# Sums of squares of k and q as products with two constant columns

## What is computed

```
q = _short_conv(x @ Wq, qc_w).reshape(b, l, NH, DK)      # NH, DK = 4, 64; ends in silu
k = _short_conv(x @ Wk, kc_w).reshape(b, l, NH, DK)
beta = jax.nn.sigmoid(x @ Wb)

def _l2norm(x):
    return x * jax.lax.rsqrt(jnp.sum(x * x, -1, keepdims=True) + 1e-06)

def _delta_rule(q, k, v, beta, chunk=CHUNK):             # chunks of 32 tokens
    q = _l2norm(q)
    k = _l2norm(k)
    v = v * beta[..., None]
    kb = k * beta[..., None]
    A = -jnp.tril(jnp.einsum('bhncd,bhned->bhnce', kb, k), -1)
    T = solve_triangular(eye - A, ...)
    ...                                                  # scan over the chunks with the state S
```

## Time and profile before

| | us |
|---|---|
| median of 3 runs | 1182.75 (1180.84 to 1190.8) |
| the profiled execution, its device time | 1176.66 |
| its span in the trace | 1174.9 |
| PE busy | 1051.7 (90%) |
| DVE busy | 827.4 (70%) |
| ACT busy | 551.9 (47%) |

### The profile page before, as it was taken

The page is one execution under the profiler, slowest core; times in us unless marked ns, Lnnn a source line. Parts: engine busy times, 40 slices in busy tenths (PEclk is TensorE's granted clock), DMA queues, the critical chain, the costliest instruction groups (busy, mean ns, idle before and its releaser), DMA issues.

```text
span 1174.9 us, 25682 instructions
## 1 busy us (share of the span) xinstructions
PE 1051.7 (90%) x10348; PEld 785.6 (67%) x10348; DVE 827.4 (70%) x1620; ACT 551.9 (47%) x989; POOL 410.6 (35%) x648
## 2 busy tenths in 40 slices
PE   5858899899999999899998998899998999897738
PEld 4734785588637885488747885488747885486427
DVE  6584478875887668875887668875887668863373
ACT  2254348443564337533575337533574337542431
POOL 7228200951058200961048300771038300770000
PEclk9779799999998999999999999999998999995779
DMA  5140104020130203110140202110040202210000
GB/s 159 20 108 1 37 19 106 4 54 2 51 77 11 45 19 86 24 36 20 33 95 1 55 19 67 42 36 20 28 99 1 54 1 64 46 36 19 1 0 19
DMA packets 82933, 47.45 MB, mean 40 GB/s; under 512 B 58496, under 2 KB 76416, under 8 KB 82816
## 3 DMA queue, kind: packets, MB, share of 16 engines
q1 hardware_dynamic: 82816, 45.82, 16.8%
HBM read 31.12 MB, written 14.68 MB: 39 GB/s over the span
## 4 chain that ended last, share of the span: by engine, by line
PE 69%; DVE 16%; ACT 8%; POOL 3%; issue 3%; DMA 1%; SPq 0%; DVEq 0%; ACTq 0%; POOLq 0%
PE psum L814 14%; PE psum L815 13%; PE psum L816 13%; PE psum L845 6%; DVE arena L1695 4%; PE psum L1007 3%; PE psum L992 3%; PE psum L1026 3%; PE psum L1031 2%; DVE arena L1701 2%; DVE arena L1735 2%; PE psum L1081 2%; PE psum L1188 2%; POOL l_prod L526 1%; POOL arena L530 1%
## 5 line engine op out<-in xcount | busy, mean ns | idle before, releaser
L526 POOL TENSOR_TENSOR l_prod<-arena 64x30 f32<-64x30 f32 (+14 forms) x240 | 143.9, 600 | 547.1 <-DMA arena<-l_dram 528.9
L601 ACT ACTIVATE h_f<-psum,b_col 128x512 f32<-128x512 f32 x128 | 88.1, 688 | 211.7 <-PE psum L816 211.5
L530 POOL TENSOR_TENSOR arena<-arena,l_prod 64x30 f32<-64x30 f32 (+14 forms) x240 | 157.7, 657 | 18.8
L814 PE MATMUL psum<-w_hi,h_hi 128*128 128x256 f32 x512 | 150.4, 294 | 0.0
L1113 PE MATMUL psum<-v_shift,fir_w 128*32 128x512 f32 x1152 | 135.5, 601 | 10.7 <-DVE fir_w L1300 10.7
L815 PE MATMUL psum<-w_lo,h_hi 128*128 128x256 f32 x512 | 144.1, 281 | 0.0
L816 PE MATMUL psum<-w_hi,h_lo 128*128 128x256 f32 x512 | 144.0, 281 | 0.0
L1409 DVE CAST h_hi<-h_f 128x512 fp32r<-128x512 f32 x128 | 63.1, 493 | 86.8 <-ACT h_f L601 43.4
L814 PE MATMUL psum<-xt_hi,w_hi 128*128 128x512 f32 x256 | 113.1, 442 | 7.5 <-DVEq L1396 5.4
L1436 DVE SCALAR_TENSOR_TENSOR conv_acc<-psum,conv_col,conv_acc 128x511 f32<-128x511 f32 x144 | 106.8, 748 | 14.6 <-ACT conv_acc L626 10.9
L845 PE MATMUL psum<-ident,arena 128*128 128x128 f32 x384 | 59.7, 302 | 57.5 <-DVE arena L1735 25.8
(11 more groups left out here) (228 smaller groups left out, 2216.3 us busy)
## 6 DMA issues: line engine op xcount, KB each, us to landing
x_in<-in_L_attn_x SPq DMA_DIRECT2D x8, 512.0 KB, 3.9
v_dram<-v_fm SPq DMA_DIRECT2D x16, 256.0 KB, 3.7
v_shift<-v_dram SPq DMA_DIRECT2D x16, 256.0 KB, 3.5
out<-x_tok SPq DMA_DIRECT2D x8, 512.0 KB, 2.8
v_shift<-v_dram SPq DMA_DIRECT2D x16, 255.5 KB, 4.3
v_shift<-v_dram SPq DMA_DIRECT2D x16, 255.0 KB, 5.1
v_shift<-v_dram SPq DMA_DIRECT2D x16, 254.5 KB, 5.7
arena<-in_L_ffn_w SPq DMA_DIRECT2D x2, 1024.0 KB, 7.2
```

The costliest lines, as they stand in the source:

```text
L526: pool.tensor_tensor(prod, l_inv[:, k + 1:, k:k + 1].broadcast_to(shape), l_inv[:, k:k + 1, 0:k].broadcast_to(shape), ALU.mult).then_inc(i ...
L530: pool.tensor_tensor(l_inv[:, k + 1:, 0:k], l_inv[:, k + 1:, 0:k], prod, ALU.add).then_inc(inverted, 1)
L601: act.activation(h_f[:, m % 2, :], bank, ACT.Gelu, bias=b1_col[:, m:m + 1]).then_inc(read, 1)
L814: pe.matmul(dst, a_hi, b_hi, start=first, stop=False, **kw)
```

## The change

The squares are taken by ACT straight from `qk_fm` in SBUF (no PSUM bank is read), feature-major. PE then multiplies them: for each tile of 128 tokens and each half, the 128x128 block of squares is the stationary operand and `pair_sel`, two constant columns (column 0 has ones in the first 64 partitions, column 1 in the last 64, zeros elsewhere), the moving one. Each product gives two of the 16 columns, token-major, in PSUM. q's turns and DVE's two reductions go; k's turns stay, since `k_tok` needs them.

k's sums go into free columns of beta's bank, behind the Gram products, and with them the bank is called full. q's sums take bank 3 alone; DVE reads them in `q_rows` and gives the bank back there.

```diff
@@ -154,7 +155,8 @@
-        q_sq = at_flat[:, 0:TILES * C].rearrange("p (u d) -> p u d", u=UNITS)
+        k_sq = sq[:, :, :]
+        q_sq = at_flat[:, 0:HALVES * T].rearrange("p (h t) -> p h t", h=HALVES)
@@ -179,7 +181,7 @@
-        Q = [("q_t", (3, 5))]
+        Q = [("q_sum", (3,))]
@@ -467,7 +469,7 @@
-                         (stat_sel, 0.0), (mean_sel, 0.0), (head_mask, 0.0)):
+                         (stat_sel, 0.0), (mean_sel, 0.0), (head_mask, 0.0), (pair_sel[:, :], 0.0)):
@@ -483,6 +485,7 @@
                 make(pool.memset(mean_sel[:, half, part], 1.0 / D))
+                make(pool.memset(pair_sel[part, half:half + 1], 1.0))
@@ -733,9 +736,9 @@
-                    for t in range(2):
-                        bank, _ = arrive(act, at, "k_t", t)
-                        act.activation(sq[:, t, :], bank, ACT.Square).then_inc(kq_squared, 1)
+                    for h in range(HALVES):
+                        act.wait_ge(silu_made, 6 * j + 3 + h)
+                        act.activation(k_sq[:, h, :], qk_fm[:, h, 0, :], ACT.Square).then_inc(kq_squared, 1)
@@ -756,13 +759,11 @@
                     silu(4)
                     silu(5)
+                    for h in range(HALVES):
+                        act.wait_ge(silu_made, 6 * j + 5 + h)
+                        act.activation(q_sq[:, h, :], qk_fm[:, h, 1, :], ACT.Square).then_inc(kq_squared, 1)
                     for h in range(2):
                         out_of(at, "fir", h, f_fm[:, h, :])
-                    for t in range(2):
-                        bank, read = arrive(act, at, "q_t", t)
-                        act.activation(at_flat[:, 512 * t:512 * t + 512], bank, ACT.Square).then_inc(kq_squared, 1)
-                        act.wait_ge(kq_squared, 4 * j + 3 + t)
-                        act.sem_inc(read, 1)
@@ -1053,8 +1054,25 @@
-                    last = pe.transpose(bank[:, 32 * t:32 * t + 32], beta_fm[:, P * t:P * t + P], ident[0:32, 0:32])
-                last.then_inc(full, 1)
+                    pe.transpose(bank[:, 32 * t:32 * t + 32], beta_fm[:, P * t:P * t + P], ident[0:32, 0:32])
+
+            def square_sums(cols, squares):
+                for t in range(TILES):
+                    for h in range(HALVES):
+                        first = HEADS * t + 2 * h
+                        last = pe.matmul(cols[:, first:first + 2], squares[:, h, P * t:P * t + P], pair_sel[:, :],
+                                         start=True, stop=True)
+                return last
+
+            def k_sums(at):
+                bank, full = where(at, "beta_t")
+                pe.wait_ge(kq_squared, 4 * at.j + 2)
+                square_sums(bank[:, TILES * 32:TILES * 32 + UNITS], k_sq).then_inc(full, 1)
+
+            def q_sums(at):
+                bank, full = claim(pe, at, "q_sum")
+                pe.wait_ge(kq_squared, 4 * at.j + 4)
+                square_sums(bank[:, 0:UNITS], q_sq).then_inc(full, 1)
@@ -1175,6 +1193,7 @@
                     k_products(at)
+                    k_sums(at)
                     projection(at, "q", 1, 1)
@@ -1198,8 +1217,7 @@
                     firs(at, 0, range(1, 9))
-                    pe.wait_ge(silu_made, 6 * j + 6)
-                    to_tok(at, "q_t", lambda h: qk_fm[:, h, 1, :])
+                    q_sums(at)
@@ -1591,12 +1609,10 @@
                     bank, read = arrive(dve, at, "beta_t")
+                    dve.tensor_scalar(nrm[:, 0, :], bank[:, TILES * 32:TILES * 32 + UNITS], 1e-6, None, ALU.add).then_inc(nrm_made, 1)
                     link(dve.tensor_copy(rows_tok[:, 1, :].rearrange("p (t h) -> p t h", t=TILES),
                                          bank[:, 0:TILES * 32].rearrange("p (t h) -> p t h", t=TILES)[:, :, 0:HEADS]))
                     dve.sem_inc(read, 1)
-                    dve.wait_ge(kq_squared, 4 * j + 2)
-                    link(dve.tensor_reduce(rows_tok[:, 0, :], sq_u, AX.X, ALU.add))
-                    dve.tensor_scalar(nrm[:, 0, :], rows_tok[:, 0, :], 1e-6, None, ALU.add).then_inc(nrm_made, 1)
@@ -1613,9 +1629,10 @@
                 def q_rows():
-                    dve.wait_ge(kq_squared, 4 * j + 4)
-                    link(dve.tensor_reduce(rows_tok[:, 2, :], q_sq, AX.X, ALU.add))
-                    dve.tensor_scalar(nrm[:, 1, :], rows_tok[:, 2, :], 1e-6, None, ALU.add).then_inc(qnrm_made, 1)
+                    bank, read = arrive(dve, at, "q_sum")
+                    dve.tensor_scalar(nrm[:, 1, :], bank[:, 0:UNITS], 1e-6, None, ALU.add).then_inc(qnrm_made, 1)
+                    dve.wait_ge(qnrm_made, j + 1)
+                    dve.sem_inc(read, 1)
```

More of the change, by code:

```diff
@@ L122, in macaron_kernel @@
         beta_fm = sb("beta_fm", [32, T])
+        pair_sel = sb("pair_sel", [P, 2])
         rows_tok = sb("rows_tok", [P, 3, UNITS])
@@ L320, in macaron_kernel @@
         T_LOADS = CPT + 2 * (CPT - 1)
-        DVE_STEPS = {"head": 43, "body": 78, "last": 73, "tail": 40}
-        CONST_MADE, C_LOADED, SETUP_DVE = 60, 57, 36
+        DVE_STEPS = {"head": 41, "body": 76, "last": 71, "tail": 40}
+        CONST_MADE, C_LOADED, SETUP_DVE = 63, 57, 36
         ZEROED, IDENT_MADE = 5, 7
```

## The result

| | before | after |
|---|---|---|
| median of 4 runs each, side by side | 1183.62 us (1180.84 to 1190.8) | 1218.19 us (1214.13 to 1219.81) |
| ratio | | 1.0277, 95% interval [1.0223, 1.0331] |
| the profiled execution, its device time | 1176.66 | 1214.13 |
| its span | 1174.9 | 1212.4 |
| mean granted clock of PE, share of 2.4 GHz | 0.940 | 0.924 |

What follows compares the result with a forecast made beforehand. PE held most of the chain, with ACT's squares and DVE's reduction pacing K and DVE's mixing pacing Q. K 8.7 + head 1.9 + bank 3 wait 10.5 = 21.1 us, forecast 1204 us (+1.8%), range 1191 to 1217.

Steps and rivals of the forecast that it cites:

- the mechanisms named: Slower because k's root waits for PE's sums behind the Gram products, and v's turns wait for DVE to free bank 3.
- Price of a product: Sums on PE: 0.105 us per instruction, 1.68 us for 16; ends 0.048 and 0.129 each.
- K's sums on the path: K stage: DVE's addition of 1e-6 waits for sums behind the Gram products; root +1.06 us in five passes.
- Where PE leads: K stage, two passes with "issue" gaps where PE is last at the logits: the full 1.68 us counts in each.
- The clock: Rival, chance 0.12: new idle makes PE's clock fall more behind DVE's ln3, +1.7 us a pass, up to 12, 1216.
- Head: Head pass: sums behind the Gram products, first four at twice the time, delay the addition by 1.9 us (0.7 to 2.4).
- Wait at bank 3: Q stage: v's turns wait until DVE's q_rows, behind the mixing, frees the bank; +1.5 us, seven passes, 10.5 us.
- the rest of q's part: Q stage: ACT's squares cost nothing, longer sums hide in PE's wait for mixing, shed DVE reduction gives nothing back.
- Tail: End of the kernel: no front half there, and three extra memsets on POOL in the set-up cost nothing.

Runs made afterwards that it cites:

- Moving the borders: Kernel after plus 16 idle two-column PE products in the head, shifting where every 256th PE instruction falls: 1200.35 us, 1.0142.
- The two kernels with both orders: Kernel after with k's sums ahead of the Gram products and q_rows within DVE's mixing, with and without 6 idle head products: 1189.86 and 1194.03 us.
- the kernel before with tiny products: Kernel before plus 12 tiny PE products behind q's turns per pass, putting every 256th PE instruction where the kernel after has it: 1184.28 us, 1.0008.
- the kernel with both orders and 6 idle products: Kernel after with k's sums ahead of the Gram products, q_rows within the mixing, and 6 idle head products: 1189.86 us, 1.0055.
- the one with 33 idle products: Kernel after plus 33 idle two-column PE products in the head, nothing changed in the passes: 1213.31 us, 1.0241.

## Why the prediction was right or wrong

**Direction: right**, by the mechanisms named. **Size: too small by 14 us**, by one mechanism that it treated wrongly and two terms that were too low. In the spans the head took 4.4 us for 1.9, the seven passes 29.0 for 19.2, the tail 3.8 for nothing. The median, 1218.19, stands 1 us above the range's upper end of 1217, and as a ratio (1.0277, against 1217/1182.75 = 1.029) just inside. That it is so near is luck: the range was that wide for a fall of the clock behind ln3, not for what happened.

- *Price of a product*, 0.105: measured 0.113 to 0.117 (1.81 and 1.87 for 16), inside its range. The forecast 1.68 for 16 was 0.1 to 0.2 low. The Trainium skill, page "TensorE: Matmul & The Clock Gate", section "Back-to-back issue gap", gives its floor of 25 ns for one multiply by itself, and says that in a stream of loads and multiplies both set the spacing; the 0.113 us agree with the second, since each product here has a new stationary operand.
- *K's sums on the path*, +1.06 a pass: +1.16 measured in the pass shown. The addition follows the Gram products by 1.9 us, and the idle before the logits shrank, as said.
- *Where PE leads*: this is the term that was mis-sized most. It took the two "issue" gaps of before as fixed places and charged the 1.68 us of the sums there. It should have asked what a gap in the Gram products costs once the chain goes through them: before, the reduction ran beside the gap; after, the sums wait behind it. Four gaps now lie on the path, and PE's clock falls behind them, 24.0 us in these four passes where the forecast for four was at most 4 x 3.2 = 13. Moving the borders gave 18 us back, and the same gaps in the order of before cost 0.08%.
- *The clock* was a rival (0.12), but at the wrong place: I looked for its fall behind ln3, and it fell behind the gaps and in the sums themselves. There are 44 us more at 1.2 GHz between the two profiles, but some 26 by the mean clocks of all runs (191 against 165). (The time at 1.2 GHz is here twice the missing share of the mean clock, times the span.) A straight line through the 69 runs of the kernel before makes an execution 0.3 us longer for each us more at 1.2 GHz. By that, as an estimate, the 26 us are worth some 8 of the 35. The two kernels with both orders have 23 to 25 us more than the kernel before beside them, worth 7 to 8, and lose 6 and 11.
- *Head*, +1.9: the root came 3.35 later and the pass ended 4.4 later. The term had the first four of 16 sums at half the clock; all 16 were.
- *Wait at bank 3*, 1.5 x 7 = 10.5: the wait was there in all seven passes, 8.5 us in total, 1.2 each. In one pass it was 0.63: DVE's mixing there took 12.9 us in place of 14.6, having started 0.5 us behind POOL's inversion and not 3.2. Freeing the bank early gave 9 to 11 us back, in the kernel after and with q's part alone alike, so the price of this wait was about right. But q's part alone, wait included, cost 4 us and not 10.5, and without the wait it was 5 us faster than before: the rest of q's part, which the prediction set at nothing, gave some 5 us back. Which piece of it did is not shown.
- *Tail*, 0: 3.8 us later. Not caused by what the change computes: the kernel before with tiny products shows 3.4 us there too, at no cost in its median. In windows of 51 us over this stretch the clock (the figure before the last two) is 0.80 before and 0.67 after, 0.70 with the tiny products. Row of before, then of after:

```profile
1097.00:1148.00 51.00, 26.49 (x145) 16.22 (x144) 27.64 (x59) 18.41 (x29) 2.77 (x4) 0.80 0.00 0
```

```profile
1131.00:1182.00 51.00, 27.64 (x138) 16.01 (x136) 27.13 (x59) 17.25 (x28) 1.98 (x3) 0.67 0.00 0
```

The profiled execution of before, 1176.66, lies under the four runs of its median, and part of the 37 us between the two profiles is that good fortune.

*Open*: how the 35 us divide exactly between idle time and clock. The two do not always move together: the kernel with both orders and 6 idle products has 190.2 us at 1.2 GHz in its trace, as many as the one with 33 idle products (190.1), no gap above 1.3 us, and a span of 1188.1 against 1212.3. So the time at the lower clock is not by itself what makes the kernel after slow; what each fall costs depends on whether the path runs over PE there, and that was not varied.

## What to carry to other kernels

A side path that looks costly on paper (turn, square, reduce on three engines) can be the safe one: it runs beside a long burst, and hides whatever stops that burst. Before work is moved onto the busiest engine behind a burst, ask what the burst's worst case is. Putting the moved work ahead of the burst gave 11 us here, with the gaps gone at the same time, but it brought a fall of the clock in every pass, and k's part stayed slower than the turn, square and reduce that it replaced in both orders (1.0119 and 1.0073). And a reader that takes over the release of a buffer has to be placed by the release, not by the read: q's part alone went from 4 us slower to 5 us faster by calling `q_rows` some 7 us earlier.

## What the runs showed of the hardware

- **Gaps at every 256th PE instruction.** Over all traces, with the Gram products right behind the turns, 25 borders fell 209 to 259 records behind their start: 24 had a gap of 1.9 to 3.0 us, one (at 213) none. Of the borders at 191 or less, one (at 191) had more than 1.3 us. With k's sums ahead of them, borders at 203, 203, 215, 215 and 239 had at most 1.3 us. 64 instructions in the head moved them all.
- **With a new 128x128 stationary operand for each, a product of two moving columns takes no less than one of 64.** 16 sums took 1.81 to 1.87 us, 0.113 to 0.117 each, a little over the 0.105 with 64 moving columns; with a stationary side of 64 columns it was 0.048. At half the clock the 16 took 3.43 to the next instruction, 0.21 each.
- **The clock fell in every pass with the sums ahead of the Gram products.** Four traces with seven passes each have a stretch at 1.2 GHz there, of 3.4 or 6.8 us; in the one kernel with the sums behind and no gap, two of seven passes have one, and in the kernel before one.
- **DVE's mixing depends on when POOL starts.** The same instructions took 14.6 us when POOL's inversion had started 3.2 us ahead of them, 14.2 at 2.3, 13.3 at 1.3 and 12.9 at 0.5. The Trainium skill, page "SBUF — State Buffer", section "SBUF: two separate sides", has VectorE (with two SBUF inputs) and GpSimd take turns at a shared pair of ports, one blocking the other for a whole instruction; these times agree in direction. So does the tail, where POOL is idle throughout the mixing: there the same instructions take 11.7 us, before and after alike, and the first three of them, in the trace of after, 3.50 us, where in passes with POOL at work they took 3.70 (0.5 us ahead) and 4.15 (2.3 us ahead):

```profile
1158.35 3.50 DVE L1712 TENSOR_TENSOR arena<-arena,mix_w 128x1024 f32<-128x1024 f32 x3
```
